# Narrow matmuls on column tiles of 32, gathered next to the value products, in a fused vision and expert-mixture kernel

## The chip, the cores and the metric

The kernel runs on one NeuronCore of a Trainium2 chip. The metric is the time of one execution on the device in microseconds (us). It was run three times; a separate execution was recorded by the hardware profiler.

## What is computed

The reference takes 64 images of 3 x 224 x 224 and 77 text tokens of 64 features for each. It cuts each image into 28 x 28 patches, embeds them, runs three graph convolutions over the grid and a projection, appends the text tokens (861 tokens of 64 features), and then applies one attention layer with 4 heads of 16 and one expert mixture, each on a layer norm and with a residual:

```python
h = p @ W_embed + b_embed + sin_positional_encoding(N, HIDDEN)[None]
for i in range(3):
    hw = h @ W_gcn[i]
    agg = (hw * snorm).at[:, dst].add(hw[:, src] * enorm)
    h = relu(agg + b_gcn[i])
h = concatenate([h @ W_out + b_out, txt], axis=1)
# attention: softmax(q k^T / 4) v per head, then @ Wo.T + bo
h = h + attention(layernorm(h))
# experts: 4 of 64 -> 128 -> 64 -> 64, the two best of each token weighted; one shared 64 -> 64 -> 128 -> 64
h = h + experts(layernorm(h))
```

## The kernel before

Images are worked on in pairs (32 pairs). The work of a pair is a list of steps; every step has a time in units of one image's attention, and all five engines walk one list, sorted by that time. So the order of work is one order written out ahead, shared by all queues, and the places (MAX, FINISH, EXPERT, PACK and so on, with different ones for the even and the odd image) set it. The list is unrolled over 16 pairs (UNROLL) and run twice, with a short list ahead of it and the rest of the second behind. Many images are in work at once: while one pair is in attention, the next ones are embedded, convolved and projected, and the ones before go through the experts.

TensorE's steps and their lines:

- `s` (L1217): scores of one head for 123 keys x 432 queries, 56 per image. ScalarE takes the exponential out of PSUM (`probs`, L889).
- `mx` (L1239): the same products the other way round, 56 per image, only for their maximum over the keys; VectorE reduces them (`neg_max_halves`, L1004).
- `pv` (L1227): the probabilities times the values of the four heads, each head on its own column tile of 32 of the array, 432 columns. A step is four products; two steps stand together, seven such blocks per image. They accumulate in PSUM banks 4 and 5.
- `embed` (L366): a quarter of a pair's patches, two images side by side on column tiles of 64, 196 columns, two accumulating halves. GpSimd packs the patches before (`xc`, L361), and VectorE adds positions after (L1018).
- `l1` (L1289): first expert layer, 432 columns at full width; `l2` (L1327): second expert layer, two experts side by side on column tiles of 64, in pieces of 492 and 369 columns, two blocks per image; the shared network's second layer (L1325) is at full width.
- `wb` (L1339) and VectorE (L1183) weight the hidden values; `l3` (L1348): third layer, the two pieces of columns side by side on tiles of 64, three accumulating products each; ScalarE copies it out (L962, L963); `back` (L1353) transposes.
- `gw`, `gagg` (L1262, L1271): graph convolution; `xt` (L1277), `qk` (L1289), `v` (L1299), `gate` (L1295), `mrow` (L1244), `ot`, `obt`, `wo` (L1305, L1310, L1316), `wt` (L1332): transposes and projections.

A product of plain float32 operands (all of `pv`, `embed`, `l2`, `l3`) becomes two weight loads and two matmuls, so a block of two `pv` steps is 16 matmuls in the profile, `embed` 8, a block of two `l2` 8, `l3` 12. The scores and maxima are in a rounded float32 form and are one each.

Every step but `pv` takes the next of six PSUM banks in turn and waits until the evacuation of the step six before it has released it. A full run of the planning, with its steps in time, is `window`:

Of the kernel before, what the change touches and what calls it, by code (L numbers as in the profile page):

```python
# [42 lines left out]
QPATCH = QROWS * GRID  # L43
# [33 lines left out]


UNROLL = 16
STACK_PARTS = 8  # L80
SLOTS = 3
WAIT = 9
# [78 lines left out]


MAX = ((-0.694, 0.158), (-0.638, 0.168))
FINISH = ((0.995, 1.063), (0.994, 1.097))
NORM_M = ((1.109, 1.257), (1.123, 1.197))
EXPERT = ((1.374, 1.997), (1.267, 1.882))
GATE = ((1.492, 1.665), (1.347, 1.379))
BIAS = ((1.602, 1.796), (1.435, 1.621))
NORM_A = ((-1.472, -1.34), (-1.504, -1.457))
PROJECT = ((-1.307, -1.281), (-1.361, -1.284))  # L170
STACK = ((-1.018, -0.911), (-1.082, -0.936))
VALUE = (-0.952, -0.989)

GRAPH = (-2.075, -1.519)
PACK = (-4.037, -3.674, -3.438, -2.779)
VGAP = 0.154
STORE = (2.456, 2.503)
FETCH = -5.787
LOAD_LEAD, EMBED_LAG = 0.117, 0.217


def image_steps(g):
# [28 lines left out]
    return out  # L211


def window(lo, hi, pairs):

    base = max(lo, 0) // 2
    placed = []
    for p in range(max(0, base - 2), min(pairs, hi // 2 + 4)):
        for t, st in pair_steps(p):
            placed.append((t, (st[0], st[1] - base, *st[2:])))  # L220
        for g in (2 * p, 2 * p + 1):
            for t, st in image_steps(g):
                placed.append((t, (st[0], st[1] - 2 * base, *st[2:])))
    placed = [(round(t - 2 * base, 6), st) for t, st in placed if lo <= round(t, 6) < hi]
    return [st for _, st in sorted(placed, key=lambda p: p[0])]


def windows(pairs):
# [60 lines left out]
def build(nc, pairs, x, txt, edges, plain, split, rows, const, out):  # L289
    ctx = ExitStack()  # L290
    with ctx:
# [10 lines left out]
        EMB = sb("embed_w", [96, 2, 64], F32)  # L302
# [60 lines left out]
        def embed_quarter(pe, T):  # L363
            for g in range(2):
                for b in range(2):
                    mm = pe.matmul(T[64 * b:64 * b + 64, 0:QPATCH], EMB[:, g, :], XCB[:, b, g, :],  # L366
                                   start=g == 0, stop=g == 1, tile_position=(0, 64 * b))
            return mm

        bo0, bo1 = ROWS["bo"]  # L370
# [826 lines left out]
        def _(pe):  # L1197
            def run(steps, base, init):
# [5 lines left out]
                for st in steps:  # L1204
# [6 lines left out]
                    mm = None  # L1211
# [61 lines left out]
                    elif kind == "xt":  # L1273
                        counted(pe, normed, nth, ("lo", st[1], st[2]))
                        for k, at in blocks_of(st[3]):
                            src = XHL[:, k, :, :].rearrange("p a f -> p (a f)")
                            mm = pe.matmul(T[:, at * PITCH:(at + 1) * PITCH], src, ident_r[0:BLK, 0:BLK + 1],  # L1277
                                           start=True, stop=True)
                    elif kind in ("qk", "l1"):
                        g = st[1]  # L1280
                        which = "a" if kind == "qk" else "m"
                        c0, cn = HALVES[st[-1]]
                        if kind == "qk" and st[2] == 0:
                            emptied(pe, turn, ("xt", g, "a", 0))
                            emptied(pe, turn, ("xt", g, "a", 1))
                        name, e, cols = ("qk", 0, 128) if kind == "qk" else \
                            (("eW1", st[2], 128) if st[2] < EXPERTS else ("sW1", 0, 128))
                        for part in (WH, WL):
                            mm = pe.matmul(T[:, 0:cn], wsplit(part, name, e, cols), XS[which][:, c0:c0 + cn],  # L1289
                                           start=part is WH, stop=part is WL)  # L1290
                    elif kind == "gate":
                        emptied(pe, turn, ("xt", st[1], "m", 0))
                        emptied(pe, turn, ("xt", st[1], "m", 1))
                        for k in range(NB):
                            mm = pe.matmul(T[0:BLK, k * 2 * EXPERTS:(k + 1) * 2 * EXPERTS],  # L1295
                                           XS["m"][:, k * BLK:(k + 1) * BLK], gsplit[:, :], start=True, stop=True)
                    elif kind == "v":
                        for k, at in blocks_of(st[2]):
                            mm = pe.matmul(T[0:BLK, at * 2 * HID:(at + 1) * 2 * HID],  # L1299
                                           XS["a"][:, k * BLK:(k + 1) * BLK], vsplit[:, :], start=True, stop=True)  # L1300
                    elif kind == "ot":
                        _, g, part = st
                        emptied(pe, turn, ("pv", g, part, 0))
                        for at, k in enumerate(out_blocks(part)):
                            mm = pe.transpose(T[0:BLK, at * 128:(at + 1) * 128], OT[:, k * BLK:(k + 1) * BLK], ident[:, :])  # L1305
                    elif kind == "obt":
                        for part in range(2):
                            emptied(pe, turn, ("ot", st[1], part))
                        for k in range(NB):
                            mm = pe.transpose(T.bitcast(BF16)[0:64, k * (BLK + 1):k * (BLK + 1) + BLK],  # L1310
                                              OB[:, k, :, :].rearrange("p h d -> p (h d)"), ident_bf[0:BLK, 0:BLK])
                    elif kind == "wo":
                        emptied(pe, turn, ("obt", st[1]))
                        for k in range(NB):
                            for part in range(3):
                                mm = pe.matmul(T[0:BLK, k * HID:(k + 1) * HID], OBT[:, k, 0:BLK], wo3[:, part, :],  # L1316
                                               start=part == 0, stop=part == 2)
                    elif kind == "l2":
                        _, g, j, t = st
                        c0, cn = PIECES[t]  # L1320
                        experts = (2 * j, 2 * j + 1) if j < 2 else (4,)
                        emptied(pe, turn, ("l1", g, experts[-1], 1))
                        for at, e in enumerate(experts):
                            if j == 2:
                                mm = pe.matmul(T[:, 0:cn], w("sW2"), H1[e % 3][:, c0:c0 + cn], start=True, stop=True)  # L1325
                            else:
                                mm = pe.matmul(T[64 * at:64 * at + 64, 0:cn], w("eW2", e, 64), H1[e % 3][:, c0:c0 + cn],  # L1327
                                               start=True, stop=True, tile_position=(0, 64 * at))
                    elif kind == "wt":
                        counted(pe, g_parts, nth, ("part2", st[1]))  # L1330
                        for k in range(NB):
                            mm = pe.transpose(T.bitcast(BF16)[0:3 * EXPERTS, k * (BLK + 1):k * (BLK + 1) + BLK],  # L1332
                                              GP[:, k, :, :].rearrange("p a e -> p (a e)"), ident_bf[0:BLK, 0:BLK])
                    elif kind == "wb":
                        _, g, j, t = st
                        c0, cn = PIECES[t]
                        if (j, t) == (0, 0):
                            emptied(pe, turn, ("wt", g))
                        mm = pe.matmul(T[:, 0:cn], select[:, 2 * j:2 * j + 2, :].rearrange("p a f -> p (a f)"),  # L1339
                                       GT[:, c0:c0 + cn], start=True, stop=True, tile_position=(SEL_ROW, 0))  # L1340
                    elif kind == "l3":
                        g = st[1]
                        emptied(pe, turn, ("l2", g, 2, 1))
                        emptied(pe, turn, ("wb", g, 1, 1))
                        for j in range(3):
                            lhs = w("eW3", j, 64) if j < 2 else w("sW3")
                            for t, (c0, cn) in enumerate(PIECES):
                                mm = pe.matmul(T[64 * t:64 * t + 64, 0:cn], lhs, H2[j][:, c0:c0 + cn],  # L1348
                                               start=j == 0, stop=j == 2, tile_position=(0, 64 * t))
                    elif kind == "back":  # L1350
                        emptied(pe, turn, ("l3", st[1]))
                        for k in range(4):
                            mm = pe.transpose(T[0:BLK, k * 128:(k + 1) * 128], OT2[:, k * BLK:(k + 1) * BLK], ident[:, :])  # L1353
# [77 lines left out]
```

## Time and profile before

| | |
|---|---|
| three runs | 4945.65 us median, 4943.49 to 4948.21 |
| profiled execution, own time | 4939.67 us |
| its span in the profile | 4937.9 us |
| mean granted TensorE clock | 0.981 of full speed |
| TensorE busy | 4719.4 us, 96% |
| VectorE, ScalarE, GpSimd busy | 65%, 60%, 34% |
| PV (L1227), busy union | 763.3 us |
| l2 (L1327), l3 (L1348), embedding (L366), busy unions | 237, 308, 113 us |

A profile counts a matmul from its start to its modelled end, and matmuls overlap; what a block costs is read from the starts of its neighbours rather than from busy times. The chain that ended last is followed back from the last instruction, and shows which engine each stretch hangs on.

### The profile page before, as it was taken

The page shows a single profiled execution, that of the slowest core. Times are in us where ns is not written, and L with a number is a line of the kernel's source. Part 1 is how long each engine was busy: PE and PEld are TensorE (multiplying, and loading weights), DVE is VectorE, ACT ScalarE, POOL GpSimd, SP SyncE. Part 2 cuts the span into 40 slices and gives each one's busy share as a digit, 9 for nine tenths or more (in the row PEclk, how much of TensorE's full clock was granted, in tenths as well). Part 3 has the DMA queues.
Part 4 walks back from the last instruction along what each step waited for, and adds up shares of the span by engine and source line. Part 5 has one row for each costly group of instructions (what it writes and reads, how often), then busy time and mean ns, then how long its engine had stood idle before and what let it go on. Part 6 is the DMA issues. An engine that isn't in the chain of part 4 may idle for free.

```text
span 4937.9 us, 80911 instructions
## 1 busy us (share of the span) xinstructions
PE 4719.4 (96%) x29262; PEld 3135.6 (64%) x29262; DVE 3206.6 (65%) x7342; ACT 2979.3 (60%) x6161; POOL 1696.6 (34%) x1681
## 2 busy tenths in 40 slices
PE   6599999999999999999999999999999999999997
PEld 4466666666666666666666666666666666666654
DVE  4366666676666666666666666667666667666663
ACT  0156666666566666666656666666666666656665
POOL 3123333334234333334333334333333333423322
PEclk8699999999999999999999999999999999999998
DMA  2433433433433432443332443333333343343220
GB/s 87 102 78 81 87 83 78 90 74 81 87 84 77 90 76 74 90 85 82 81 78 70 90 85 82 80 81 75 82 86 82 80 88 74 83 85 74 34 48 6
DMA packets 193397, 385.98 MB, mean 78 GB/s; under 512 B 74986, under 2 KB 118634, under 8 KB 193002
## 3 DMA queue, kind: packets, MB, share of 16 engines
q1 hardware_dynamic: 191978, 379.91, 34.2%
q8 instruction: 237, 3.88, 0.4%
q14 instruction: 158, 1.29, 0.1%
q10 hardware_dynamic: 1024, 0.89, 0.1%
HBM read 309.13 MB, written 109.26 MB: 85 GB/s over the span
## 4 chain that ended last, share of the span: by engine, by line
PE 74%; DVE 11%; ACT 7%; issue 2%; DMA 2%; POOL 1%; ACTq 0%; SPq 0%; DVEq 0%; another core or an unknown queue 0%; POOLq 0%
PE ps L1227 15%; PE ps L1217 13%; PE ps L1239 12%; PE ps L1271 9%; DVE neg_max_halves L1004 8%; PE ps L1289 6%; PE ps L1327 4%; ACT probs L889 4%; PE ps L1348 3%; PE ps L1262 3%; PE ps L366 2%; PE ps L1277 2%; PE ps L1316 2%; PE ps L1295 1%; DMA image_rows<-image_by_row 1%
## 5 line engine op out<-in xcount | busy, mean ns | idle before, releaser
L1004 DVE TENSOR_REDUCE neg_max_halves<-ps 123x1 f32<-123x432 f32 (+1 forms) x3584 | 2000.9, 598 | 766.9 <-PE ps L1239 751.9
L889 ACT ACTIVATE probs<-ps 123x432 f32<-123x432 f32 x3584 | 1690.9, 542 | 663.7 <-PE ps L1217 626.8
L1239 PE MATMUL ps<-k_stack,q_stack 96*123 96x432 f32 x3584 | 1293.5, 396 | 38.5 <-DMA k_stack<-qk_scratch 22.3
L1217 PE MATMUL ps<-q_stack,k_stack 97*123 97x432 f32 x3584 | 1253.1, 395 | 52.6 <-ACT probs L889 12.5
L1239 PEld LDWEIGHTS ps<-k_stack,q_stack 96*123 96x123 f32 x3584 | 638.7, 186 | 419.1 <-issue 273.2
L1217 PEld LDWEIGHTS ps<-q_stack,k_stack 97*123 97x123 f32 x3584 | 641.8, 186 | 340.1 <-issue 107.7
L1227 PE MATMUL ps<-probs,v_and_one 123*32 123x432 f32 x7168 | 763.3, 540 | 1.6 <-ACT probs L889 1.6
L952 ACT ACTIVATE hidden<-ps,plain_w 128x432 f32<-128x432 f32 x640 | 400.2, 634 | 148.2 <-PE ps L1289 148.2
L1271 PE MATMUL ps<-adjacency,parts_hi 112*128 112x392 f32 x1344 | 463.5, 345 | 3.5 <-DVE parts_lo L1026 3.4
L1271 PE MATMUL ps<-adjacency,parts_lo 112*128 112x392 f32 x1344 | 459.8, 342 | 0.0
L815 POOL TENSOR_TENSOR nodes_T<-nodes_T,dinv_row 128x392 f32<-128x392 f32 x128 | 130.8, 1023 | 846.4 <-ACT nodes_T L901 845.3
L1227 PEld LDWEIGHTS ps<-probs,v_and_one 123*32 123x32 f32 x7168 | 182.5, 110 | 353.5 <-issue 287.2
L820 POOL TENSOR_TENSOR centred_and_squared<-tokens,ln_stats_m 123x448 f32<-123x448 f32 x64 | 59.9, 936 | 980.0 <-DVE ln_stats_m L1058 980.0
L852 POOL TENSOR_TENSOR moe_T<-gate_weights,bias_rows 123x448 f32<-123x448 f32 x256 | 242.9, 949 | 311.9 <-DVE gate_weights L1160 283.3
L1043 DVE TENSOR_TENSOR nodes_T<-ps,dinv_row 128x392 f32<-128x392 f32 x192 | 108.4, 565 | 323.3 <-PE ps L1271 323.3
L857 POOL TENSOR_TENSOR tokens<-tokens,moe_T 123x448 f32<-123x448 f32 x256 | 292.6, 1143 | 32.4
L820 POOL TENSOR_TENSOR centred_and_squared<-tokens_next,ln_stats_a 123x448 f32<-123x448 f32 x64 | 59.9, 935 | 674.7 <-DVE ln_stats_a L1058 674.7
L361 POOL COPY patch_columns<-image_rows 96x392 f32<-96x392 f32 x256 | 235.3, 948 | 94.1 <-DMA image_rows<-image_by_row 73.4
L958 ACT ACTIVATE hidden<-ps,plain_w 128x492 f32<-128x492 f32 (+1 forms) x384 | 234.1, 634 | 51.7 <-PE ps L1327 43.7
L1271 PEld LDWEIGHTS ps<-adjacency,parts_hi 112*128 112x128 f32 x1344 | 255.3, 190 | 6.2 <-issue 3.9
L1262 PE MATMUL ps<-plain_w,nodes_T 128*112 128x128 f32 (+2 forms) x1792 | 243.2, 278 | 14.8 <-POOL nodes_T L815 6.8
L1271 PEld LDWEIGHTS ps<-adjacency,parts_lo 112*128 112x128 f32 x1344 | 255.4, 190 | 1.6
(158 smaller groups left out, 6118.3 us busy)
## 6 DMA issues: line engine op xcount, KB each, us to landing
image_rows<-image_by_row SPq DMA_DIRECT2D x256, 586.9 KB
q_stack<-qk_scratch SPq DMA_DIRECT2D x256, 216.0 KB, 7.9
k_stack<-qk_scratch SPq DMA_DIRECT2D x256, 216.0 KB, 9.1
image_by_row<-in_x SPq DMA_DIRECT2D x192, 196.0 KB
qk_scratch<-parts_hi SPq DMA_DIRECT2D x64, 432.0 KB, 2.9
qk_scratch<-parts_lo SPq DMA_DIRECT2D x64, 432.0 KB, 3.7
out<-tokens SPq DMA_DIRECT2D x64, 215.2 KB
tokens_next<-in_txt SPq DMA_DIRECT2D x64, 19.2 KB
```

Of the source, the lines that this page charges most:

```text
L361: return pool.tensor_copy(XCB[:, b, :, :].rearrange("p g (i j) -> p g i j", j=GRID), src)
L852: ins = pool.tensor_tensor(TMP[:, :, :], GW[:, :, e:e + 1].to_broadcast(shape), row("eb3", e).unsqueeze(1).to_broadcast(shape), ALU.mult)
L857: ins = pool.tensor_tensor(hb, hb, TMP[:, :, :], ALU.add)
L889: act.activation(P[:, (g * 2 * NB + unit) % SLOTS, h, :], T[0:BLK, 0:HW], ACT.Exp, scale=SCALE).then_inc(free[r], 1)
L952: act.activation(H1[e % 3][:, c0:c0 + cn], T[:, 0:cn], ACT.Relu, bias=bias).then_inc(free[r], 1)
L1004: v.tensor_reduce(NM[:, qb * HEADS + h, half:half + 1], T[0:BLK, 0:keys], AX.X, ALU.max, negate=True).then_inc(free[r], 1)
L1217: mm = pe.matmul(T[0:BLK, 0:cn], KS[:, g % 2, h, kb * BLK:(kb + 1) * BLK], QS[:, g % 2, h, c0:c0 + cn], start=True, stop=True)
L1227: pm = pe.matmul(acc[32 * h:32 * h + 32, half, 0:HW], VV[:, g % 2, kb, h, :], P[:, slot, h, :], start=kb == 0, stop=kb == NB - 1, tile_pos ...
L1239: mm = pe.matmul(T[0:BLK, 0:cn], QS[0:SHIFT_ROW, g % 2, h, qb * BLK:(qb + 1) * BLK], KS[0:SHIFT_ROW, g % 2, h, c0:c0 + cn], start=True, st ...
L1262: mm = pe.matmul(T[0:m, at * 128:(at + 1) * 128], HT[:, k * size:k * size + m], rhs, start=True, stop=True)
L1271: mm = pe.matmul(T[:, 0:GHALF], part[:, k, :], adj[:, k, half * GHALF:(half + 1) * GHALF], start=k == 0 and part is UH, stop=k == NG - 1 a ...
L1289: mm = pe.matmul(T[:, 0:cn], wsplit(part, name, e, cols), XS[which][:, c0:c0 + cn], start=part is WH, stop=part is WL)
```

## The change

The embedding, both l2 blocks and l3 are put on column tiles of 32 as PV is: each product on a tile of 64 becomes two on tiles of 32 with half the weights' columns each and the same moving data. A new function, `gathered`, goes through the sorted list and moves each block of these steps to stand directly behind or ahead of the nearest `pv`, at most 60 steps (REACH) away, unless a step of the kinds named in NARROW lies between. The places are set anew.

```diff
 UNROLL = 16
+REACH = 60
...
-FINISH = ((0.995, 1.063), (0.994, 1.097))
-NORM_M = ((1.109, 1.257), (1.123, 1.197))
-EXPERT = ((1.374, 1.997), (1.267, 1.882))
+FINISH = ((0.981, 1.071), (0.994, 1.097))
+NORM_M = ((1.109, 1.389), (1.123, 1.197))
+EXPERT = ((1.374, 1.997), (1.267, 1.883))
 GATE = ((1.492, 1.665), (1.347, 1.379))
-BIAS = ((1.602, 1.796), (1.435, 1.621))
-NORM_A = ((-1.472, -1.34), (-1.504, -1.457))
-PROJECT = ((-1.307, -1.281), (-1.361, -1.284))
-STACK = ((-1.018, -0.911), (-1.082, -0.936))
-VALUE = (-0.952, -0.989)
+BIAS = ((1.602, 1.796), (1.435, 1.532))
+NORM_A = ((-1.472, -1.364), (-1.504, -1.457))
+PROJECT = ((-1.335, -1.281), (-1.361, -1.284))
+STACK = ((-1.018, -0.93), (-1.082, -0.936))
+VALUE = (-0.858, -0.984)
...
-PACK = (-4.037, -3.674, -3.438, -2.779)
+PACK = (-4.153, -3.674, -3.438, -2.779)
...
-FETCH = -5.787
-LOAD_LEAD, EMBED_LAG = 0.117, 0.217
+FETCH = -5.683
+LOAD_LEAD, EMBED_LAG = 0.117, 0.166
...
+NARROW = {"embed": ("embed", "xc", "hs", "load"), "l2": ("l1", "l2", "l3", "wb"), "l3": ("l1", "l2", "l3", "wb", "hb", "back")}
+
+
+def gathered(steps):
+
+
+    def narrow(st):
+        return st[0] in NARROW and st[:3:2] != ("l2", 2)
+
+    def distance(at, by, kinds):
+
+        n = 0
+        while 0 <= at < len(steps) and n < REACH:
+            if steps[at][0] == "pv":
+                return n
+            if steps[at][0] in kinds:
+                return None
+            at, n = at + by, n + 1
+        return None
+
+    steps, i = list(steps), 0
+    while i < len(steps):
+        if not narrow(steps[i]):
+            i += 1
+            continue
+        j = i
+        while j < len(steps) and narrow(steps[j]) and steps[j][:3] == steps[i][:3]:
+            j += 1
+        block, kinds = steps[i:j], NARROW[steps[i][0]]
+        back, ahead = distance(i - 1, -1, kinds), distance(j, 1, kinds)
+        if back is not None and (ahead is None or back <= ahead):
+            steps[i - back:j] = block + steps[i - back:i]
+        elif ahead is not None:
+            steps[i:j + ahead] = steps[j:j + ahead] + block
+        i = j
+    return steps
...
-    return [st for _, st in sorted(placed, key=lambda p: p[0])]
+    return gathered(st for _, st in sorted(placed, key=lambda p: p[0]))
...
-                    mm = pe.matmul(T[64 * b:64 * b + 64, 0:QPATCH], EMB[:, g, :], XCB[:, b, g, :],
-                                   start=g == 0, stop=g == 1, tile_position=(0, 64 * b))
+                    for c in (0, 32):
+                        at = 64 * b + c
+                        mm = pe.matmul(T[at:at + 32, 0:QPATCH], EMB[:, g, c:c + 32], XCB[:, b, g, :],
+                                       start=g == 0, stop=g == 1, tile_position=(0, at))
...
-                                mm = pe.matmul(T[64 * at:64 * at + 64, 0:cn], w("eW2", e, 64), H1[e % 3][:, c0:c0 + cn],
-                                               start=True, stop=True, tile_position=(0, 64 * at))
+                                continue
+                            for c in (0, 32):
+                                mm = pe.matmul(T[64 * at + c:64 * at + c + 32, 0:cn], w("eW2", e, 64)[:, c:c + 32],
+                                               H1[e % 3][:, c0:c0 + cn], start=True, stop=True,
+                                               tile_position=(0, 64 * at + c))
...
-                                mm = pe.matmul(T[64 * t:64 * t + 64, 0:cn], lhs, H2[j][:, c0:c0 + cn],
-                                               start=j == 0, stop=j == 2, tile_position=(0, 64 * t))
+                                for c in (0, 32):
+                                    mm = pe.matmul(T[64 * t + c:64 * t + c + 32, 0:cn], lhs[:, c:c + 32],
+                                                   H2[j][:, c0:c0 + cn], start=j == 0, stop=j == 2,
+                                                   tile_position=(0, 64 * t + c))
```

## Rows read from the trace of the kernel before

**Rows 1.** The page: busy time and share of TensorE; the chain that ended last, by engine.
```profile
PE 4719.4 (96%) x29262; PEld 3135.6 (64%) x29262; DVE 3206.6 (65%) x7342; ACT 2979.3 (60%) x6161; POOL 1696.6 (34%) x1681
...
PE 74%; DVE 11%; ACT 7%; issue 2%; DMA 2%; POOL 1%; ACTq 0%; SPq 0%; DVEq 0%; another core or an unknown queue 0%; POOLq 0%
```
**Rows 2.** Busy time by stage, one pair: stretch, length, PE, PEld, DVE, ACT, POOL, clock, DMA.
```profile
2000.00:2146.60 146.60, 143.86 (x905) 95.77 (x904) 98.68 (x228) 92.89 (x193) 52.35 (x53) 1.00 0.36 82
```
**Rows 3.** Groups of instructions, whole span: count, busy us, mean ns, idle before.
```profile
L1227 PE MATMUL ps<-probs,v_and_one 123*32 123x432 f32 x7168 | 763.3, 540 | 1.6 <-ACT probs L889 1.6
L366 PE MATMUL ps<-patch_columns,embed_w 96*64 96x196 f32 x1024 | 113.4, 342 | 11.3 <-POOL patch_columns L361 11.3
L1227 PEld LDWEIGHTS ps<-probs,v_and_one 123*32 123x32 f32 x7168 | 182.5, 110 | 353.5 <-issue 287.2 <-ACT probs L889 61.4
...
L1004 DVE TENSOR_REDUCE neg_max_halves<-ps 123x1 f32<-123x432 f32 (+1 forms) x3584 | 2000.9, 598 | 766.9 <-PE ps L1239 751.9
```
**Rows 4.** Order of time on PE around a lone embedding: start us, length us, line.
```profile
2083.63 0.36 PE L1217 MATMUL ps<-q_stack,k_stack 97*123 97x432 f32 x1
2083.92 0.88 PE L366 MATMUL ps<-patch_columns,embed_w 96*64 96x196 f32 x8
...
2085.04 0.36 PE L1239 MATMUL ps<-k_stack,q_stack 96*123 96x432 f32 x1
```
**Rows 5.** Order of time on PE: around a PV block; then half of another.
```profile
2089.13 0.36 PE L1289 MATMUL ps<-x_stack_moe,split_lo 128*128 128x432 f32 x1
...
2091.30 0.37 PE L1289 MATMUL ps<-x_stack_moe,split_hi 128*128 128x432 f32 x1
...
2053.44 0.91 PE L1227 MATMUL ps<-probs,v_and_one 123*32 123x432 f32 x8
```
**Rows 6.** Order of time on PE: l2 ahead of an embedding, and of PV.
```profile
2031.23 1.67 PE L1327 MATMUL ps<-hidden,plain_w 128*64 128x492 f32 x8
2032.73 0.84 PE L366 MATMUL ps<-patch_columns,embed_w 96*64 96x196 f32 x8
...
2101.33 1.67 PE L1327 MATMUL ps<-hidden,plain_w 128*64 128x492 f32 x8
2102.93 1.66 PE L1227 MATMUL ps<-probs,v_and_one 123*32 123x432 f32 x16
```
**Rows 7.** Order of time around l3: PE, a second run on PE, then ACT.
```profile
2117.70 0.66 PE L1239 MATMUL ps<-k_stack,q_stack 96*123 96x432 f32 x2
...
2120.73 1.81 PE L1227 MATMUL ps<-probs,v_and_one 123*32 123x432 f32 x16
...
2055.31 0.44 PE L1217 MATMUL ps<-q_stack,k_stack 97*123 97x432 f32 x1
...
2058.35 0.57 PE L1227 MATMUL ps<-probs,v_and_one 123*32 123x432 f32 x4
...
2117.83 0.57 ACT L962 ACTIVATE moe_T<-ps 64x492 f32<-64x492 f32 x1 [3.65 <-PE ps L1348]
...
2118.91 2.65 ACT L889 ACTIVATE probs<-ps 123x432 f32<-123x432 f32 x6
```
**Rows 8.** Pieces of the chain in this pair: start, length, what.
```profile
2051.16 0.81 PE ps L366 x8
...
2142.54 0.82 PE ps L366 x8
```
**Rows 9.** Order of time on PE: an output projection.
```profile
2136.86 1.34 PE L1316 MATMUL ps<-wo_parts,attn_bf_T 65*123 65x64 bf16 x21
```
**Rows 10.** Order of time: packing ahead of [rows 4]; weighting ahead of l3, and l3.
```profile
2077.16 1.91 POOL L361 COPY patch_columns<-image_rows 96x392 f32<-96x392 f32 x2
...
2111.17 2.13 DVE L1183 TENSOR_TENSOR hidden<-ps,hidden 128x492 f32<-128x492 f32 x4
...
2115.09 2.69 PE L1348 MATMUL ps<-hidden,plain_w 128*64 128x492 f32 x12
```
**Rows 11.** Order of time on PE: value products that wait, idle before in brackets.
```profile
2073.38 0.54 PE L1299 MATMUL ps<-v_hi_lo,x_stack_attn 128*123 128x128 f32 x3 [0.52 <-ACT probs L889]
```

More of the change, by code:

```diff
@@ L1325, in run @@
                                 mm = pe.matmul(T[:, 0:cn], w("sW2"), H1[e % 3][:, c0:c0 + cn], start=True, stop=True)
-                            else:
-                                mm = pe.matmul(T[64 * at:64 * at + 64, 0:cn], w("eW2", e, 64), H1[e % 3][:, c0:c0 + cn],
-                                               start=True, stop=True, tile_position=(0, 64 * at))
+                                continue
[3 more added lines that the diff above has]
+                                               tile_position=(0, 64 * at + c))
                     elif kind == "wt":
```

## Prediction

> **What bounds the kernel now.** I read the busy times first: TensorE is busy for 96% of the span; the chain that ended last runs through TensorE for 74% [rows 1]. The reader is to see that TensorE's queue is the bound, but not a bare one: 18% of the chain lies on VectorE and ScalarE, which empty the PSUM banks. In the steady state one pair of images takes 146.6 us, at a granted clock of 1.00 [rows 2], so no clock effect is in play. Of these, I put some 11 us down to the queue waiting for a bank, by adding up how far the score and maximum products stand apart beyond their usual 0.20 us; the run of twelve in [rows 7] is the pattern: 2120.73 - 2117.70 = 3.03 us for 2.4 us of columns, and 0.1 us each for leaving and entering narrow tiles, so 0.4 us of waiting.
>
> Then I read TensorE's order of time around the narrow blocks (values PV, embedding, second layer l2, third layer l3), since the change touches these and the places of the rest.
>
> **The price of a change of tile size.** A full-width product of 432 columns starts 0.20 us after the one before it. In [rows 4] a lone embedding stands between two wide products: from the start of the last wide one (2083.63) to that of the second wide one behind it (2085.04) are 1.41 us. Two wide products are 0.40. The embedding's own columns are four rounds (a round is one matmul on every tile side by side): in [rows 6], where it follows a block of its own size, eight matmuls take 0.84 and one takes 0.34 [rows 3], so three rounds are 0.50 and four 0.66. What is left is 0.35 us: the array empties before the first narrow product, its first weights load in the open, and much of both again on the way out. The same sum for a value block [rows 5]: 2.17 from 2089.13 to 2091.30, less 0.40, less four rounds of 0.36 (0.91 for two rounds, less 0.53 for one matmul, as 0.54 is the mean of its group [rows 3], and 0.02 for the side-by-side starts), gives 0.33. I take 0.35 for a visit to narrow tiles that disappears.
>
> Going from tiles of 64 to tiles of 32 without a wide product between is not free either. In [rows 6] l2 is followed by PV after 1.60 us, but by an embedding of its own tile size after 1.50; and that embedding takes 0.84 where the lone one of [rows 4] takes 0.88. The seam costs 0.10 + 0.04 = 0.14 us.
>
> **How many of these go.** I wrote out the step lists of both versions from the planning functions. Before: 735 runs of narrow products (448 PV blocks, 287 of tiles of 64), 33 of them directly followed by one of the other size, so 702 returns to full width. After, with one tile size: 578 runs and 578 returns. In one pair of the steady state that is 23 runs against 18. What merges in each pair: three of four embeddings now stand directly ahead of or behind a PV block, and so does l3 of one image; the l2 block that already stood ahead of PV loses its change of size. The fourth embedding leaves an l2 block and joins a PV block, which saves nothing. Both first l2 blocks, one second and one l3 stay alone, because a step of their own chain that may not be crossed keeps them from the nearest PV.
> - 702 - 578 = 124 visits gone, at 0.35: 43.4 us.
> - The other 33 of the 735 - 578 = 157 entries gone, at 0.14: 4.6 us.
> - Together 48.0 us. All merged blocks lie on the chain (the four embedding and l3 blocks of a pair; the first and the last in [rows 8]), so the cost itself is on the path.
>
> **The columns themselves.** A block of 64 split into two tiles of 32 streams the same columns on four tiles where it streamed them on two, side by side. The PV rows show that four tiles go at one round per 432 columns x 2 / 2.4 GHz = 0.36 us, and two tiles of 64 go at the same rate (l2, two rounds of 492 and two of 369 columns, 2 x 0.41 + 2 x 0.31 = 1.44 of the 1.50 in [rows 6]). So l2 and l3 keep their 0.41 and 0.31 us rounds; their four weight loads per round (0.11 each at 32 columns, by [rows 3], side by side) fit, as they do in PV. Two more starts in a round, at the 0.02 / 3 = 0.007 us used above, only shift its end. I cost this at nothing. TensorE gets 2 x (1,024 + 1,024 + 768) = 5,632 more instructions (weight loads and matmuls), hidden as long as the queue's supply keeps ahead.
>
> Where that could fail is the embedding: its four rounds of 0.164 now hold 16 pairs of load and matmul, one per 0.041 us. The output projection shows 21 pairs in 1.34 us, (1.34 - 0.22) / 20 = 0.056 us a pair [rows 9]. If that is the supply's pace, an embedding takes 16 x 0.056 = 0.90 in place of 0.66, and 124 of them cost 30 us. The other end is nothing: in [rows 5] the first two rounds of PV come at their column time, eight pairs, with all weight loads ready. The queue holds work issued ahead while the wide products, 0.20 us each, run, and three of four embeddings stand next to a PV block, which needs only one pair per 0.09 us. I take nothing, nearer to the PV rows, and keep 30 for the range.
>
> On this point the Trainium skill ("TensorE: Matmul & The Clock Gate", section "Wait — 56ns, not 53.3ns?") speaks against the change: it gives some 62 ns per MATMUL for a stream decoded in microcode, which would make 16 x 0.062 = 0.99 us of an embedding, an estimate of 41 us more over 124, and take nearly all of the gain. The 0.056 a pair of [rows 9] shows that this chip's stream can go at least a little faster than that; no row shows a long stretch below it.
>
> **What the new places add.** A block moves for all engines, so its evacuation moves too. The embeddings come sooner after their packing. The tightest one is at 2083.92; GpSimd's packing ended at 2079.07 [rows 10], 4.8 us ahead. EMBED_LAG falls by 0.051 image (3.7 us), the gathering gives some back; by the step list and these durations it is 1.8 us earlier, so 3.0 us stay. l3 moves back over three products (0.6 us) to PV, and VectorE's last product for it (L1183) ended at 2113.30, 1.8 us ahead of 2115.09 [rows 10]: 1.2 stay. No wait there. Nothing is moved past a queue of SP's or GpSimd's transfers so that they would be late: loads and stacks shift by under 2 us against tens.
>
> But the score and maximum products, which those blocks used to separate, now stand in longer runs. Such a run needs a bank emptied every 0.20 us, while ScalarE takes 0.44 for one (six in 2.65) and VectorE some 0.56 (0.598 is the mean of its group [rows 3]), so up to 0.28 per product when the two alternate. In [rows 7] ScalarE idles 3.65 us across the PV and l3 blocks, and then has two evacuations (1.1 us) and six scores behind each other. Directly after the moved l3, fifteen such products stand in a row where twelve did, after the other l3 twelve instead of nine, around the last embedding eight instead of five, and in two more places one to three more: about twelve products a pair more in long runs. The measured waits in such runs are 0.44 us over 12 and, where 11 stand from 2055.31 to 2058.35, 3.04 - 2.2 - 0.1 = 0.74: 0.04 to 0.07 each. At 0.045, twelve give 0.54 us a pair, 17 us in all. Bounds: nothing, and 0.28 - 0.20 = 0.08 each, 31 us.
>
> The sum: -48 + 17 = -31 us on the span of 4937.9, so 4907; the profiled execution itself took 4939.7, which gives 4909. It lies 6.0 below the median of the three runs, 4945.65; on that footing 4915.
>
> **The rivals.**
> 1. *More than forecast, below 4900.* The new places shorten waits as well: the value products L1299 wait for ScalarE at 2073.38, 0.52 us of idle time [rows 11], and the new order puts these products behind a PV block, when banks are free. At one such wait a pair it is 32 x 0.5 = 16 us. That and no cost of longer runs: 4946 - 48 - 16 = 4882 at best. Against it: the work of ScalarE around there stays the same.
> 2. *No change, about 4946.* Either the supply of instructions binds the embeddings (+30: 4915 + 30 = 4945), or the time saved on TensorE comes back as bank waits, since VectorE and ScalarE carry 18% of the chain. For it: the 0.056 a pair of [rows 9]; against: the merged blocks lie where the chain is on TensorE. The skill's figure above belongs here, and would give 4915 + 41 = 4956.
> 3. *Slower, about 4965.* The longer runs decide alone. A PV block and l3 back to back keep banks idle for 4.1 us, and everything that ScalarE owes comes in one bunch. It decides from 48 / 32 = 1.5 us of added waits a pair; at 0.1 us a product, more than the bound of 0.08 for evacuations that alternate, since scores come in bunches, over 20 products a pair, 2.1 us, it would be +19. For it: the 3.65 us idle in [rows 7]. Against: the two long runs of [rows 7] show 0.04 and 0.07.
> 4. *The change does nothing:* the seam between PV and a merged block still drains although both are tiles of 32. The embedding behind l2 (1.50, no drain) speaks against it; it is part of the no-change case.
>
> **How the numbers follow.** Forecast (4900 to 4935, the 31 us with 0 to 31 of added waits, plus a little): 0.62. Below 4900: 0.12. No change, 4936 to 4955 (0.2%, about what this kernel's times can tell from none): 0.13. Slower than that: 0.13. So faster 0.74, same 0.13, slower 0.13. The range leaves out about one in ten on each side: 4890 to 4952.
>
> **What the changed profile would show.** The lone embedding's 1.41 us shrinks to about 0.67 between its start and that of the PV block behind it; a merged l3 starts about 1.45 us after its PV block; embeddings' matmuls, now 2,048, keep 0.33 us each and four rounds within 0.67 (if the supply binds, 0.9). The pair takes about 145.6 us. The waits of VectorE and ScalarE on L1239 and L1217 rise a little. It is wrong if the stretches behind l3 take over 1 us more a pair than now, or if the embeddings stretch.

## The result, and the profile after

The changed kernel takes 5059.9 us (median of five runs, 5056.5 to 5065.8) against 4945.65: ratio 1.024, 95% interval 1.0227 to 1.0252. It is 114 us slower where 31 us less were forecast. The page of its profiled execution, to be read beside [rows 1]: busy times, the granted clock in 40 slices, the chain by engine.

```profile
span 5063.5 us, 86543 instructions
...
PE 4815.9 (95%) x32078; PEld 3198.8 (63%) x32078; DVE 3217.0 (64%) x7342; ACT 2988.6 (59%) x6161; POOL 1697.9 (34%) x1681
...
PEclk8689999999999999999999999999999999999988
...
PE 69%; DVE 14%; ACT 9%; issue 3%; DMA 2%; POOL 1%; ACTq 0%; SPq 0%; DVEq 0%; POOLq 0%
```

The slices hide what matters, since a tenth is too coarse; the mean granted clock tells it: 0.955, where it was 0.981. VectorE and ScalarE now hold 23% of the chain for 18%.

First, does a merge do what was forecast? TensorE's order of time around an embedding that now stands ahead of a PV block, beside [rows 4] and [rows 5]:

```profile
2091.90 0.35 PE L1259 MATMUL ps<-q_stack,k_stack 97*123 97x432 f32 x1
2092.19 0.87 PE L408 MATMUL ps<-patch_columns,embed_w 96*32 96x196 f32 x16
2092.87 1.64 PE L1269 MATMUL ps<-probs,v_and_one 123*32 123x432 f32 x16
2094.44 0.47 PE L1331 MATMUL ps<-x_stack_moe,split_hi 128*128 128x432 f32 x1
2094.75 0.36 PE L1331 MATMUL ps<-x_stack_moe,split_lo 128*128 128x432 f32 x1
```

It does: PV starts 0.68 us after the embedding, its column time, and four rounds with 16 pairs of load and matmul keep their pace. From 2091.90 to 2094.75 are 2.85 us for 0.40 (two wide products) + 0.66 (embedding) + 1.44 (PV) = 2.50 of columns, so one visit's price of 0.35 for both blocks.

Then where do 125.6 us of span (5063.5 - 4937.9) go? I took the start of every fourteenth PV block in both traces, one pair of images. The first is 26.8 us late; the pair in which the second list ends takes 17.7 us more (172.1 for 154.4); the other 30 pairs together 80.4 more, and the end 0.7. Of the 30, the first and the last take 12.1 of the 80.4. The 28 between them, the steady pairs, are of two kinds: 8 take 146.1 us, a little less than the 146.3 of most pairs before, and 20 take about 150.4. What tells them apart is the clock: each of the 20 has a stretch of 10.2 us at a granted clock of 0.50, and none of the 8 has. One such place, TensorE's order of time and the busy time by stretch (length, PE, PEld, DVE, ACT, POOL, clock, DMA):

```profile
779.28 1.25 PE L1281 MATMUL ps<-k_stack,q_stack 96*123 96x432 f32 x5
780.37 0.49 PE L1347 MATMUL ps<-ident_r,attn_T 128*123 128x128 f32 x3
...
781.97 0.46 PE L1259 MATMUL ps<-q_stack,k_stack 97*123 97x432 f32 x1
782.48 0.46 PE L1281 MATMUL ps<-k_stack,q_stack 96*123 96x432 f32 x1
783.01 0.97 PE L1259 MATMUL ps<-q_stack,k_stack 97*123 97x432 f32 x2
784.15 0.72 PE L1281 MATMUL ps<-k_stack,q_stack 96*123 96x432 f32 x1 [0.17 <-DVE attn_bf L1134]
...
788.34 2.39 PE L1358 MATMUL ps<-wo_parts,attn_bf_T 65*123 65x64 bf16 x21
```
```profile
780.80:784.20 3.40, 2.99 (x12) 1.47 (x10) 3.33 (x10) 1.22 (x3) 0.00 (x0) 0.99 1.06 129
784.20:794.40 10.20, 10.20 (x52) 7.16 (x56) 5.38 (x11) 4.62 (x9) 1.04 (x2) 0.50 0.86 95
794.40:804.60 10.20, 9.83 (x71) 5.21 (x67) 4.92 (x11) 8.04 (x18) 5.56 (x6) 1.00 0.18 63
```

Scores and maxima, 0.20 us apart elsewhere, stand 0.5 apart: TensorE waits for banks that VectorE (busy 3.33 of 3.40) empties. At 784.2 the granted clock falls to 0.50, which is 1.2 GHz, for 10.2 us, and TensorE's work in them takes nearly twice its time: the 21 pairs of the output projection take 2.39 us for 1.34 in [rows 9]. The first pair, the list's end pair and the last pair have the same fall at this place, so there are 23 in all. The column that reads "PE busy" shows 2.99 of 3.40 ahead of the fall and would not have told, since a matmul counts up to its modelled end.

### The profile page after: what moved, and what is told of

The parts are those of the page before. It is cut to its first block, busy times and chain, and to the rows that moved or that the text cites. A ratio compares the mean times of both kernels' runs of the same rounds, so it can differ in the third digit from the quotient of the medians.

```text
span 5063.5 us, 86543 instructions
## 1 busy us (share of the span) xinstructions
PE 4815.9 (95%) x32078; PEld 3198.8 (63%) x32078; DVE 3217.0 (64%) x7342; ACT 2988.6 (59%) x6161; POOL 1697.9 (34%) x1681
## 4 chain that ended last, share of the span: by engine, by line
PE 69%; DVE 14%; ACT 9%; issue 3%; DMA 2%; POOL 1%; ACTq 0%; SPq 0%; DVEq 0%; POOLq 0%
PE ps L1269 14%; PE ps L1259 11%; DVE neg_max_halves L1046 10%; PE ps L1281 10%; PE ps L1313 9%; PE ps L1331 6%; ACT probs L931 5%; PE ps L1370 4%; PE ps L1393 3%; PE ps L1304 3%; PE ps L1358 2%; PE ps L408 2%; PE ps L1319 2%; ACT hidden L1000 2%; DMA image_rows<-image_by_row 1%
## 5 line engine op out<-in xcount | busy, mean ns | idle before, releaser
L1259 PE MATMUL ps<-q_stack,k_stack 97*123 97x432 f32 x3584 | 1291.8, 409 | 77.3 <-SPq L803 39.4
L1281 PEld LDWEIGHTS ps<-k_stack,q_stack 96*123 96x123 f32 x3584 | 657.8, 190 | 398.8 <-issue 232.5
L1259 PEld LDWEIGHTS ps<-q_stack,k_stack 97*123 97x123 f32 x3584 | 662.0, 191 | 380.4 <-DVE neg_max_halves L1046 99.4
L1269 PE MATMUL ps<-probs,v_and_one 123*32 123x432 f32 x7168 | 781.4, 551 | 13.5 <-ACT probs L931 13.5
L1269 PEld LDWEIGHTS ps<-probs,v_and_one 123*32 123x32 f32 x7168 | 197.6, 112 | 366.6 <-issue 268.9
L1068 DVE TENSOR_TENSOR parts_lo<-ps,parts_hi 112x512 fp32r<-112x512 f32 x192 | 116.4, 620 | 227.6 <-ACT parts_hi L938 227.6
```

The source lines that it names most:

```text
L1259: mm = pe.matmul(T[0:BLK, 0:cn], KS[:, g % 2, h, kb * BLK:(kb + 1) * BLK], QS[:, g % 2, h, c0:c0 + cn], start=True, stop=True)
L1269: pm = pe.matmul(acc[32 * h:32 * h + 32, half, 0:HW], VV[:, g % 2, kb, h, :], P[:, slot, h, :], start=kb == 0, stop=kb == NB - 1, tile_pos ...
L1281: mm = pe.matmul(T[0:BLK, 0:cn], QS[0:SHIFT_ROW, g % 2, h, qb * BLK:(qb + 1) * BLK], KS[0:SHIFT_ROW, g % 2, h, c0:c0 + cn], start=True, st ...
```

## The experiments

Ratios are to runs of the kernel before on the same chip. Its medians in the four sets of experiments lie between 4939.3 and 4944.2 us, so a difference of two medians from different sets is good to some 6 us only. A "steady pair" below is one of the 28 as above, and its time is that of the pairs in which the clock doesn't fall, where nothing else is said.

**Four kernels that take the change apart.** `return gathered(...)` against `return list(...)`, the block of places from MAX to EMBED_LAG of one version or the other, and the tiles.

`e1_tiles_only`: the tiles of 32 alone.
```diff
-    return gathered(st for _, st in sorted(placed, key=lambda p: p[0]))
+    return list(st for _, st in sorted(placed, key=lambda p: p[0]))
... and all places as before
```


> The kernel before with only the tiles of 32 in embedding, l2 and l3; its own places, no gathering. Theory P (the new places make a stretch with too little work on TensorE, whose clock then falls to 1.2 GHz for some 10 us in two of three pairs): 4941 to 4947, for only the 33 changes of size from 64 to 32 go (-4.6 us). Theory T (the doubled instructions of the tiles of 32 slow TensorE): most of the 115 us, 5030 to 5060. Theory G (the gathering makes the waits): as P.

4939.7 us, ratio 0.9993 (0.9984 to 1.0002): nothing that can be told from no change, -2.8 by the medians. The doubled instructions cost nothing. A steady pair takes 146.2 us; 11 of the 28 have a fall of the clock for 3.4 us and take 147.6.

`e2_tiles_gather`: the changed kernel with all places as before.


> Tiles of 32 and the gathering, with the places of before. Theory P: no 10 us stretches at 1.2 GHz; 4900 to 4940, the gain of the merged visits less new bank waits. Theory G (gathering lengthens the runs of scores and maxima, TensorE waits there and the clock falls): low stretches in most pairs, 5020 to 5060. Theory T: 5030 or more.

4968.3 us, 1.0050 (1.0033 to 1.0066), clock 0.98. No stretches of 10 us in the steady pairs, only 3.4 us in 8 of them, as in 7 of the kernel before. But it is slower, 147.6 us as the mean of the 28 pairs for 146.7 in `e1_tiles_only`: theory P is right on the clock and wrong on the gain.

`e3_no_gather`: the changed kernel with `list` for `gathered`.


> The changed kernel without the gathering: tiles of 32 and the new places. Theory P: the low stretches stay, 5040 to 5110 (the merged visits come back, +40). Theory G: none, 4940 to 4960. Theory T: 5060 to 5100.

4995.9 us, 1.0108 (1.0093 to 1.0123). Slower by 53, but all 28 steady pairs take 146.8 us and have no low stretches, which theory P had not expected. Most of the 53 us are the late start and the end of the list (first PV block at 269.2, 170.2 us for the list's end pair), which are thus the places' work.

`e4_places_only`: the kernel before with the new places.


> The kernel before with only the new places; tiles of 64, no gathering. Theory P: low stretches in most pairs, 5040 to 5110, about as the changed kernel without gathering. Theories G and T: 4940 to 4960.

5026.7 us, 1.0169 (1.0154 to 1.0184). The late start again (269.8), and low stretches in a few of the steady pairs (22 of 28 are free of them). So neither the places nor the gathering alone gives the steady fall of the clock; the new places bring it in a few pairs with the old tiles, in none with tiles of 32, and in most with the gathering on top.

**Four kernels on the three suspected costs of the places.** Each is the changed kernel with one edit.

`f1_pack0`:
```diff
-PACK = (-4.153, -3.674, -3.438, -2.779)
+PACK = (-4.11, -3.674, -3.438, -2.779)
```


> The changed kernel with the first quarter's packing 0.043 image later (PACK[0] -4.11 for -4.153), so that the load of the second quarter no longer falls into the last dozen steps of the first and the second list, at whose ends every engine waits until all transfers of the list have landed. Theory L (these two waits are the 27 us by which the first PV block is late and the 18 us at the second list's end): 5015 to 5030, the first PV block back near 241 us. Rival (the lateness comes of the lists' other contents): 5050 or more. The low clock in the pairs stays.

5037.6 us, 1.0198 (1.0183 to 1.0213): 22 us of the loss are back, less than expected. The longest waits of the transfers' queue (SP) and of TensorE on SP in the changed kernel (us in total, times, longest):
```profile
SPq L786 <- DMA q_stack<-qk_scratch: 42.6, 2, 21.4
```
```profile
PE ps L1259 <- SPq L803: 19.7, 1, 19.7
```
and SP's in `f1_pack0`:
```profile
SPq L786 <- DMA q_stack<-qk_scratch: 17.8, 2, 9.0
```
This is the wait at the two lists' ends, 12 us shorter each. The list's end pair takes 158.4 us for 172.1, and the first PV block starts at 254.1 for 267.5. It is still 13 late. The reason is in GpSimd's order of time in the changed kernel's first list:
```profile
119.76 1.70 POOL L401 COPY patch_columns<-image_rows 96x392 f32<-96x392 f32 x2 [10.80 <-DMA image_rows<-image_by_row]
121.50 1.97 POOL L853 TENSOR_TENSOR nodes_T<-embedded_T,dinv_row 128x392 f32<-128x392 f32 x2
```
The packing of the next pair's first quarter waits for its image, and the first step of the graph convolution (`hs`, L853) stands behind it, for which TensorE waits 19.0 us. In the list of before, `hs` comes first; at -4.11 it doesn't yet.

`f2_value`: VALUE = (-0.952, -0.989) as before.


> The changed kernel with the value products' place of before (VALUE). Theory V (moving v out from between the transposes of the attention's output leaves a stretch in which TensorE mostly waits for banks, after which its clock falls): low stretches mostly gone, 4970 to 5000. If FINISH does it: 5050 to 5065.

5042.5 us, 1.0212 (1.0197 to 1.0227). The low stretches are still there, 280 us of them in all behind the first 300 us, for 311 in the changed kernel. So theory V falls as the cause, though the time lies in neither range. 15 steady pairs have a fall for 20, and in 6 of them it lasts 13.7 us for 10.2. The value products' place does bear on the clock, by 17 us in all.

`f3_finish`: FINISH = ((0.995, 1.063), (0.994, 1.097)) as before.


> The changed kernel with the place of before for the attention's output steps (FINISH). If the spread of ot, obt and wo makes the weak stretch: low stretches mostly gone, 4970 to 5000. Theory V: 5050 to 5065.

4963.7 us, 1.0049 (1.0032 to 1.0066), 96 less than the changed kernel. That is the 23 falls at some 4.2 us each: no 10 us stretch is left in the steady pairs, and they take 145.9 us. The list's end pair takes 167.9 for 172.1. In the changed kernel the attention's output steps start 0.014 image earlier and are spread wider. Seven scores and maxima stand between `obt` and `wo` there where four stood, and six for five ahead of `obt`, so the 21 pairs of `wo` come later.

`f4_filler`: the changed kernel with work added in the weak stretch, six products (FILL = 6) in each pair.
```diff
+                        if part == 1 and g % 2 == 0:
+                            for _ in range(FILL):
+                                pe.matmul(T[:, 0:GHALF], adj[:, 0, 0:128], adj[:, 0, 0:GHALF], start=True, stop=True)
                         emptied(pe, turn, ("pv", g, part, 0))
```


> The changed kernel with six more wide products of 392 columns (1.0 us of columns), whose result is overwritten, ahead of the second ot of each even image, where the weak stretch begins: added work, nothing else. Theory P, that the loss in the pairs is the low clock: the 10 us stretches go, and the time falls by up to 24 x 4 = 96 us less up to 32 us for the added work, 4965 to 5030. Rival (the waits cost the time and the clock costs nothing): 5060 to 5095.

4966.4 us, 1.0053 (1.0038 to 1.0068): with 192 matmuls more it is 94 us faster than the changed kernel. The same place, order of time on TensorE and the busy time by stretch:
```profile
768.41 0.44 PE L1282 MATMUL ps<-k_stack,q_stack 96*123 96x432 f32 x1
768.74 1.33 PE L1348 MATMUL ps<-adjacency 112*128 112x392 f32 x6
769.91 0.60 PE L1351 MATMUL ps<-ident_r,attn_T 128*123 128x128 f32 x4
```
```profile
768.70:772.10 3.40, 3.21 (x17) 2.51 (x16) 3.33 (x9) 1.10 (x3) 0.00 (x0) 1.00 1.03 126
```
The clock stays at 1.00 and the pair takes 146.1 us. That settles it: waits of the same kind with a little more columns among them cost nothing more, and the loss in the pairs was the clock.

**Do the causes add, and what is the gathering worth?** The next three share the kernel `g1_fin_pack`, the changed one with FINISH and PACK[0] (-4.037) of before.

`g1_fin_pack`:


> The changed kernel with FINISH and PACK[0] of before: the first undoes the weak stretch, the second puts the packing of the next pair's first quarter back behind hs in the first list (GpSimd waited there for its image with the graph convolution behind it) and its load behind the lists' ends. If the three causes add: 4964 less 27 at the start less 13 at the list's end, 4918 to 4930, faster than both kernels. If the start and the end hang on other places: 4945 to 4965.

4926.2 us, 0.9967 (0.9956 to 0.9979), faster than both kernels. They add: first PV block at 245.5 (TensorE waits 6.5 us for `hs`, for 19.0), the list's end 153.6, a steady pair 145.9. One of the 28 still has a fall of 10.2 us and takes 150.3.

`h1_fin_pack_no_gather`: `list` for `gathered`.


> The same as the kernel with FINISH and PACK[0] of before, without the gathering: 124 visits to narrow tiles come back. By the visits' price alone 43 us more, about 4967. By the theory that merged blocks give most of it back in waits for banks (1.1 of 1.4 us a pair): 10 us more, 4930 to 4945.

4949.9 us, 1.0017 (1.0008 to 1.0025). The gathering is worth 24 us here, about half of its visits' price.

`h2_gather_embed`: `narrow` returns `st[0] == "embed"`.


> The same, but only the embeddings are gathered, l2 and l3 are not (611 visits in place of 578). By the visits' price alone 12 us more than with all gathered. If it is l3 behind PV that makes the waits (4.1 us in which no bank is filled), no more or less: 4915 to 4930.

4913.4 us, 0.9941 (0.9928 to 0.9953), the fastest of all, 13 us under `g1_fin_pack` with 33 visits more. A pair takes 145.7 for the 146.8 of `h1_fin_pack_no_gather`: 1.1 us for three visits, the full price. In the order of the steady pair the l3 of the even image is the only difference; TensorE around it, first with l3 moved up to PV (`g1_fin_pack`), then not, each with VectorE's reductions behind it:
```profile
2110.16 1.66 PE L1269 MATMUL ps<-probs,v_and_one 123*32 123x432 f32 x16
2111.63 2.65 PE L1393 MATMUL ps<-hidden,plain_w 128*32 128x492 f32 x24
2114.21 1.24 PE L1281 MATMUL ps<-k_stack,q_stack 96*123 96x432 f32 x5
...
2118.60 1.31 PE L1269 MATMUL ps<-probs,v_and_one 123*32 123x432 f32 x12
...
2114.71 4.72 DVE L1046 TENSOR_REDUCE neg_max_halves<-ps 123x1 f32<-123x432 f32 x9 [3.96 <-PE ps L1281]
```
```profile
2109.18 1.66 PE L1269 MATMUL ps<-probs,v_and_one 123*32 123x432 f32 x16
2110.77 0.86 PE L1281 MATMUL ps<-k_stack,q_stack 96*123 96x432 f32 x3
2111.55 2.67 PE L1393 MATMUL ps<-hidden,plain_w 128*32 128x492 f32 x24
...
2117.20 1.82 PE L1269 MATMUL ps<-probs,v_and_one 123*32 123x432 f32 x16
...
2111.27 1.63 DVE L1046 TENSOR_REDUCE neg_max_halves<-ps 123x1 f32<-123x432 f32 x3 [1.50 <-PE ps L1281]
2114.65 3.36 DVE L1046 TENSOR_REDUCE neg_max_halves<-ps 123x1 f32<-123x429 f32 x6 [1.75 <-PE ps L1281]
```
From PV to PV it is 8.44 us against 8.02. l3 starts 1.47 us after PV, as forecast, but the three maxima that stood between them kept VectorE in work during l3 (1.63 us). Without them it sits idle for 3.96 us and then owes nine reductions in a row, 4.72 us, and TensorE waits for their banks. Saved 0.35, paid 0.77.

`g4_before_filler`: the kernel before with the filler of `f4_filler`, a control.


> The kernel before with the six added wide products of the filler, a control: what the filler costs where the clock hardly falls. If it lies in waits for banks, nothing to +10 us; if in the open, +32. A gain would say that the filler helps by something else than by keeping the clock.

4943.3 us, 1.0000 (0.9991 to 1.0010). 192 matmuls of 392 columns, 31 us of columns in all, cost nothing: they lie in the waits. And they gain nothing where the clock holds through this stretch. The falls of 3.4 us stay, in 7 of the 28 pairs as in the kernel before; they stand at another place, taken up below.

**Three more, on what was open.**

`k1_old_places_embed`: tiles of 32, places of before, only the embeddings gathered.


> Tiles of 32, the places of before, only the embeddings gathered: 611 visits for 702. If l2 and l3 bring the waits, the visits' price comes out: 4940 - 91 x 0.35 = 4908, so 4903 to 4920. If the embeddings bring them: 4945 or more.

4946.3 us, 1.0006 (0.9997 to 1.0015). No gain with 91 visits less, which is the second branch of what was expected. A steady pair takes 146.6 for 146.2 in `e1_tiles_only`, but 3 have a 3.4 us fall for 11, so the mean of the 28 is 146.8 for 146.7.

`k2_old_places_l`: the same with only l2 and l3 gathered.


> Tiles of 32, the places of before, only l2 and l3 gathered: 640 visits for 702, -22 us by their price. The l3 of the odd image moves ahead over fourteen products, past an embedding, to stand right before PV, the other right behind PV. If these bring the waits: 4950 to 4985. If the embeddings do: 4915 to 4930.

4945.5 us, 1.0004 (0.9994 to 1.0013). A pair takes 146.7. This lies in neither range, and the two runs don't single out a culprit: with the old places each half gives back all that it saves (5 to 6 us slower than `e1_tiles_only` by the ratios, hardly clear of noise), and both together lose 28.

`k3_after_embed_only`: the changed kernel with only the embeddings gathered.


> The changed kernel with only the embeddings gathered, all its new places kept. The low stretches came with new places and gathering together. If the moved l3 is what tips it: 4955 to 4975, no 10 us stretches. If the embedding ahead of the PV block shortly before the weak stretch does: 5030 to 5055.

5076.4 us, 1.0267 (1.0253 to 1.0281), outside both ranges and slower than the changed kernel, with the low stretches in 24 of the 28 steady pairs. The moved l3 isn't what tips the clock.

## Why the prediction was wrong, point by point

- *"At a granted clock of 1.00 [rows 2], so no clock effect is in play."* This is the step that failed most. The clock was 1.00 in the pair that I read, but the mean of 0.981 said that it isn't always. The wait of TensorE behind VectorE between the output's transposes was in the kernel before already, and the clock held through it; the new FINISH thinned this stretch, and the clock fell there 23 times, in 20 of 28 steady pairs, at about 4.2 us each. Undone by FINISH (96 us) or by added work (94 us).
  The kernel before had falls too, at another place: 7 of its 28 steady pairs take 147.8 us for 146.3, each with 3.4 us at half the clock, some 9 us behind `obt`. There TensorE waits for ScalarE around the value products, as in [rows 11], here with the slowed PV block (3.10 us for 1.66):
```profile
1193.28 1.06 PE L1217 MATMUL ps<-q_stack,k_stack 97*123 97x432 f32 x2 [0.35 <-ACT probs L889]
1194.27 3.10 PE L1227 MATMUL ps<-probs,v_and_one 123*32 123x432 f32 x16
```
  No kernel with the new place of these products has a fall of 3.4 us in a steady pair, and every kernel with the old one and FINISH of before has some. So the changed kernel gave up one weak stretch, worth about 10 us, and got a worse one. That was the right half of the rival "more than forecast", though not by the mechanism it names.
- *"Nothing is moved past a queue ... so that they would be late: loads and stacks shift by under 2 us against tens."* Wrong for PACK[0]. 0.116 image is 8.5 us, and it moved a load ahead of both lists' ends, where all transfers must have landed, and a packing ahead of `hs` in GpSimd's first list. That is most of the 26.8 + 17.7 = 44.5 us of the span at these two places, which I had not looked at. From `f3_finish` to `g1_fin_pack`, where PACK[0] is the only difference, the first PV block comes 23.2 us earlier and the list's end pair takes 14.3 less, 37.5 together; 4.2 of the 44.5 is a fall of the clock in the list's end pair. In `g1_fin_pack` 4.8 and -0.8 are left of the two.
- *"At 0.045, twelve give 0.54 us a pair."* Near in size with the new places, and the reason was only partly right. From `h1_fin_pack_no_gather` to `g1_fin_pack` 43.4 us of visits go and 23.7 are gained, so 19.7 come back, 0.6 a pair. But not as a cost of every longer run: the three merges of embeddings give their full price, and the moved l3 alone costs 0.77. What counts there is whether VectorE is fed during PV and l3. With the places of before (`e1_tiles_only` to `e2_tiles_gather`) 28 us are lost where 43.4 should be gained, so 2.2 us a pair come back.
- *The new places themselves* had no term of their own in the sum. Without gathering a steady pair takes 146.8 us with them (`e3_no_gather`) for 146.3 before.
- *The price of a visit, 0.35, and their count:* right. 22 full visits a pair became 18 in the trace, three embeddings' merges gave 1.1 us a pair in `h2_gather_embed`.
- *The seam from 64 to 32, 0.14 each:* too small to tell; -2.8 us measured for -4.6, within the interval of no change.
- *The columns at nothing, and the supply of instructions:* right. The embedding's rounds kept 0.17 us with four pairs in each, 0.042 a pair; the 62 ns per matmul of the Trainium skill ("TensorE: Matmul & The Clock Gate", section "Wait — 56ns, not 53.3ns?") does not bind here, nor does the 0.056 of [rows 9].
- *The sum for the steady pair:* -1.0 us forecast, -0.2 measured where the clock holds; 0.5 of the difference is the new places.
- *The rivals:* the slower one named the wrong mechanism. Waits behind l3 are real, but alone they only eat half of the gain; the slowness is from the clock and from the lists' ends, which no rival had. The two signs of being wrong didn't show it either: from PV to PV around the moved l3 it is 8.5 us for 8.0, not over 1 us more, and the embeddings kept their pace.

What stays open: why the same merges of embeddings save 1.1 us a pair with the new places and lose 0.4 with the old ones; the order of maxima and scores around each differs, but that was not taken apart. Not known either is which new place costs the 0.5 us by which a pair without gathering is longer (146.8 for 146.3), and how a little less work on TensorE tips the clock in one kernel and not in its neighbour: `f3_finish` waits in the same stretch and keeps 1.00. In one kernel, too, the same order of steps has the fall in 20 pairs and not in 8, and no run shows why.

## What to carry to other kernels

Before moving work away from a stretch, ask whether it is what keeps TensorE's clock up there; a stretch that costs nothing as a wait can cost 4 us as a clock, and a few useless matmuls in it are a cheap test and even a cure. A step order is also judged at its seams: at the ends of unrolled lists, where all transfers must have landed, and at the start, where a queue's first wait holds all behind it. And a wide block of work on the bounding engine should be placed so that the engines that empty its banks have their queues full when it begins.

## What was not expected of the hardware

- A fall of the granted clock to 0.50 lasted 10.2 us in the changed kernel, with TensorE busy for all 10.20 by the profile, while the falls in the steady pairs of the kernel before lasted 3.4 us. Each of the long ones made its pair some 4.2 us longer, each of the short ones 1.5.
- Leaving the full array for narrow column tiles and coming back costs 0.35 us around an embedding, 0.33 around PV, and 0.35 around both together; narrow blocks of one tile size pass into one another at their column time (0.68 us from an embedding to PV, 1.47 from PV to l3).
